# An adaLN transformer block on one core: the opening's loads on two queues, its first products by feature halves, and seven block products for one more head

## The reference

```python
ada = cond @ ada_w + ada_b                       # six 256-wide chunks per sequence
x1 = layernorm(x) * (1 + scale1) + shift1
q, k, v = split(x1 @ qkv_w + qkv_b)              # 16 heads of 128
a = softmax(q @ k.T / sqrt(128)) @ v
y = x + gate1 * (a @ out_w + out_b)
h = gelu((layernorm(y) * (1 + scale2) + shift2) @ ffn_w1 + ffn_b1)
z = y + gate2 * (h @ ffn_w2 + ffn_b2)
hn = rms_norm(square(relu(z @ ternary(W_fc).T)))
out = x + hn @ ternary(W_proj).T
```

## Time and profile before

| | |
|---|---|
| median of 3 runs | 350.53 us (349.86 to 351.02) |
| profiled execution | 350.69 us, span 348.9 us |
| TensorE busy | 342.3 us, 98% of the span |
| VectorE busy | 222.4 us, 64% |
| ScalarE busy | 220.2 us, 63% |
| GpSimd busy | 148.7 us, 43% |
| mean DMA rate | 47 GB/s over the span |

### The profile page before, as it was taken

The page is one execution under the profiler, slowest core; times in us unless marked ns, Lnnn a source line. Parts: engine busy times, 40 slices in busy tenths (PEclk is TensorE's granted clock), DMA queues, the critical chain, the costliest instruction groups (busy, mean ns, idle before and its releaser), DMA issues.

```text
span 348.9 us, 5879 instructions
## 1 busy us (share of the span) xinstructions
PE 342.3 (98%) x1950; PEld 293.7 (84%) x1950; DVE 222.4 (64%) x386; ACT 220.2 (63%) x560; POOL 148.7 (43%) x140
## 2 busy tenths in 40 slices
PE   8999999999999999999999999999999999999995
PEld 7888888889888888888888888888787788889884
DVE  6676756553555664456466454585875788577796
ACT  2773565667576657756664675667579536876593
POOL 3571329736534964644595573479341100000000
PEclk9999999999999999999999999999999999999998
DMA  6953003100300320030020002020000000000002
GB/s 176 362 192 120 3 0 120 62 1 3 120 0 0 120 60 0 0 120 0 25 95 0 0 6 115 0 62 0 4 0 2 0 2 0 0 2 1 1 32 90
DMA packets 12338, 16.53 MB, mean 47 GB/s; under 512 B 720, under 2 KB 8992, under 8 KB 12320
## 3 DMA queue, kind: packets, MB, share of 16 engines
q1 hardware_dynamic: 12136, 16.16, 14.2%
q10 hardware_dynamic: 184, 0.15, 0.1%
HBM read 15.25 MB, written 1.05 MB: 47 GB/s over the span
## 4 chain that ended last, share of the span: by engine, by line
PE 74%; issue 20%; DVE 3%; ACT 1%; POOL 1%; POOLq 0%; ACTq 0%
PE bank L1228 16%; PE bank L1230 16%; PE bank L1229 16%; PE bank L1315 8%; PE bank L1298 8%; PE bank L1304 4%; PE bank L1427 2%; PE bank L1442 1%; DVE yT L976 1%; DVE yT L966 1%; PE bank L1463 1%; PE bank L1422 1%; DVE yT L962 0%; ACT prob L579 0%; ACT hbuf L718 0%
## 5 line engine op out<-in xcount | busy, mean ns | idle before, releaser
L391 POOL TENSOR_TENSOR prob<-prob,rinv 128x512 f32<-128x512 f32 x32 | 36.2, 1131 | 60.3 <-DVE rinv L1025 59.9
L579 ACT ACTIVATE prob<-bank,negmax 128x128 f32<-128x128 f32 x128 | 45.4, 365 | 25.6 <-DVE negmax L1012 25.6
L1315 PEld LDWEIGHTS bank<-probT,vals 128*128 128x128 f32 x256 | 33.3, 191 | 3.2 <-issue 0.8
L952 DVE SCALAR_TENSOR_TENSOR o_lo<-bank,bias,o_hi 128x512 fp32r<-128x512 f32 x32 | 23.9, 745 | 17.2 <-ACT o_hi L532 17.2
L532 ACT ACTIVATE o_hi<-bank,bias 128x512 fp32r<-128x512 f32 x32 | 21.9, 686 | 19.4 <-PE bank L1315 19.4
L1315 PE MATMUL bank<-probT,vals 128*128 128x128 f32 x256 | 33.9, 275 | 0.0
L350 POOL TENSOR_TENSOR wqk_lo<-raw_qk,wqk_hi 128x512 fp32r<-128x512 f32 x16 | 21.2, 1323 | 19.6 <-ACT wqk_hi L493 18.1
L488 POOL TENSOR_TENSOR xr<-raw_qk,xt 128x256 f32<-128x256 f32 x1 | 0.7, 721 | 67.2 <-ACT raw_qk L796 67.2
L1012 DVE TENSOR_REDUCE negmax<-bank 128x4 f32<-128x512 f32 x32 | 21.8, 682 | 7.9 <-PE bank L1298 7.9
L1228 PE MATMUL bank<-wv_hi,x_hi 128*128 128x512 f32 x62 | 26.1, 420 | 0.0
L579 ACT ACTIVATION_READ_ACCUMULATOR prob<-bank,negmax 128x1 f32 x128 | 26.0, 203 | 0.0
(11 more groups left out here) (218 smaller groups left out, 974.1 us busy)
## 6 DMA issues: line engine op xcount, KB each, us to landing
raw_qk<-in_L_cond_qkv_w_dram SPq DMA_DIRECT2D x6, 512.0 KB, 4.6
raw_v<-in_L_cond_qkv_w_dram SPq DMA_DIRECT2D x4, 512.0 KB, 4.1
raw_o<-in_L_cond_out_w_dram SPq DMA_DIRECT2D x4, 512.0 KB, 3.5
t_w<-in_L_cond_ada_w_dram SPq DMA_DIRECT2D x1, 1024.0 KB, 8.9
raw_w<-in_L_cond_ffn_w_dram SPq DMA_DIRECT2D x2, 512.0 KB, 6.9
t_raw<-in_L_ffn_W_fc_dram SPq DMA_DIRECT2D x4, 256.0 KB, 3.7
t_raw<-in_L_ffn_W_proj_dram SPq DMA_DIRECT2D x4, 256.0 KB, 3.8
raw_qk<-in_L_cond_ffn_w_dram SPq DMA_DIRECT2D x1, 1024.0 KB, 4.9
```

Source lines behind the costliest of these rows:

```text
L391: nc.gpsimd.tensor_tensor(e, e, rinv[:, j % 2, :].unsqueeze(2).broadcast_to([P, SQ, P]), ALU.mult).then_inc(norm_done, 1)
L579: e = nc.scalar.activation(prob[:, j % 2, s, :], bank[BS][:, s * P:(s + 1) * P], ACT.Exp, bias=negmax[:, j % 2, s:s + 1], accum_out=rowsum ...
L952: nc.vector.scalar_tensor_tensor(out=lo[:, :], in0=bank[BO][:, :], scalar=bias[:, bass.ds(HG * G + VB + j % HG, 1)], in1=hi[:, :].bitcast( ...
L1315: m = nc.tensor.matmul(bank[BO][:, s * P:(s + 1) * P], vals[:, b, h], probT[:, s, :], start=True, stop=True)
```

## The change

The three parts:

1. **Opening.** The second half of quad 0's x is loaded from ScalarE's queue, and the bias rows too; SyncE then waits for the first half alone. The identity matmuls go from 5 + 7 + 3 to 5 + 3 + 1, and TensorE transposes all bias rows before the conditioning product. Transposes come by feature half (k = 1 first), VectorE modulates sequences 0 and 1 and ScalarE sequences 2 and 3 of each half, and queries and keys of head 0 are made together, half by half. One of two `wv_lo` parts and one of two copies of raw x move to VectorE.
2. **First group.** Head 2's queries and keys are made by the seven products. `weight_sums` takes two heads at once, `x_sums` moves ahead of unit (0, 1), and the two `x_sums_lo` stand together.
3. **End of attention.** The addition of x becomes `add_x`, a step of its own, announced by half. For quad 1 the gate, the addition and the transposes are spread over later chunks; `transpose_y` goes half by half.

```diff
         @block.sync
-            for h in range(2):
-                s = slice(h * SQ // 2, (h + 1) * SQ // 2)
-                sp.dma_start(xt[:, s, :], x[s].rearrange("b t d -> t b d")).then_inc(x0_in[h], 16)
+            sp.dma_start(xt[:, 0:SQ // 2, :], x[0:SQ // 2].rearrange("b t d -> t b d")).then_inc(x0_in[0], 16)
             sp.dma_start(ada_w1, ada_w[:, 0:2 * D].rearrange("(k p) n -> p k n", p=P)).then_inc(ada1_in, 16)
-            sp.wait_ge(x0_in[1], 16)
+            sp.wait_ge(x0_in[0], 16)
...
         @block.gpsimd
             pool.wait_ge(xs_lo, KD)
-            for k in range(KD):
-                wv_lo_part(k, k + 1)
+            wv_lo_part(0, 1)
             wqk_lo_part(1, 2)
...
-            weight_sums(0, 3, 4, 0)
+            weight_sums(0, 2, 4, 0)
...
         @block.scalar
+            act.dma_start(xt[:, SQ // 2:SQ, :], x[SQ // 2:SQ].rearrange("b t d -> t b d")).then_inc(x0_in[1], 16)
             act.dma_start(crow, cond).then_inc(cond_in, 16)
             act.dma_start(arow, ada_b.rearrange("(n p) -> n p", p=P)).then_inc(arow_in, 16)
+            for src, at, n in ((qkv_b, QB, 3 * H), (out_b, OB, KD), (ffn_b1, F1B, NC), (ffn_b2, F2B, KD)):
+                act.dma_start(brow[at - NA:at - NA + n, :], src.rearrange("(n p) -> n p", p=P)).then_inc(bias_in, 16)
...
         @block.vector
+            def modulate_first():
+                dve.wait_ge(ada_ready, 1)
+                for k, src, full, hi in ((1, bank[BO], m1_d, hi1_d), (0, bank[BV], mod_d, hi0_d)):
+                    dve.wait_ge(xt0_done, KD - k)
+                    for b in range(SQ // 2):
+                        m = nc.vector.tensor_scalar(xq0[:, k, b * P:(b + 1) * P], src[:, b * P:(b + 1) * P],
+                                                    ada[:, SCALE1 + k, b:b + 1], ada[:, SHIFT1 + k, b:b + 1], ALU.mult, ALU.add)
+                    m.then_inc(full, 1)
+                    dve.wait_ge(full, 1)
+                    nc.vector.tensor_copy(x_hi[:, k, 0:SQ // 2 * P], xq0[:, k, 0:SQ // 2 * P]).then_inc(hi, 1)
...
-            modulate(0, SHIFT1, SCALE1, bank[0:2])
-            dve.wait_ge(small_cp, 4)
+            modulate_first()
+            dve.wait_ge(wv_h, 2)
+            nc.vector.tensor_tensor(wv_lo[:, 1, :], raw_v[:, 1, :], wv_hi[:, 1, :].bitcast(F32), ALU.subtract).then_inc(wv_l, 1)
+            dve.wait_ge(xraw_mm, 1)
+            nc.vector.tensor_copy(xT[:, 1, cols(0)], bank[BS][:, :]).then_inc(xT1_done, 1)
+            dve.wait_ge(small_cp, 3)
             keep_q0(0, 0, 1)
...
                 if c == 1:
                     accumulate(NU - 1, NG - 1, 1, last=True)
+                if c == 2:
                     gate_y(1)
-                if c == 5:
+                if c == 3:
+                    add_x(1)
+                if c == 6:
                     dve.wait_ge(gt_mm, 2)
                     stats_of(3)
...
         @block.tensor
+            def first_qk():
+                dsts = (bank[BQ], bank[BK])
+                pe.wait_ge(wqk_h, 1)
                 for k in (1, 0):
...
-            ada_product(GATE1 + 4, GATE1 + 6, ada_w2, bank[7])
             pe.wait_ge(q1_done, 1)
             pe.wait_ge(k1_done, 1)
-            qk_products(2, 0, 0)
+            pair_p1(0, 2)
+            pair_p2(0, 2)
+            ada_product(GATE1 + 4, GATE1 + 6, ada_w2, bank[7])
+            pair_p6(0, 2)
+            pair_p5(0, 2)
+            pair_p7(0, 2)
             ada_product(GATE1 + 6, GATE1 + 8, ada_w2, bank[7])
-            pe.wait_ge(q1_done, 2)
-            pe.wait_ge(k1_done, 2)
-            qk_products(2, 0, 1, (BE, BY))
+            pair_p4(0, 2)
+            pair_p3(0, 2)
```

More of the change, by code:

```diff
@@ L524, in modulate @@
                 hi_part(x_hi[:, 0, cols(quad)], xf[:, 0, :], xs_hi)
-                if e:
-                    act.wait_ge(mod_d, e + 1)
-                    hi_part(x_hi[:, 1, cols(quad)], xfull[:, 1, :], xs_hi)
+                act.wait_ge(mod_d, e + 1)
+                hi_part(x_hi[:, 1, cols(quad)], xfull[:, 1, :], xs_hi)
+            def modulate_first():
+                act.wait_ge(ada_ready, 1)
+                for k, src, full, hi in ((1, bank[7], m1_a, hi1_a), (0, bank[6], mod_a, xs_hi)):
+                    act.wait_ge(xt0_done, KD - k)
+                    for b in range(SQ // 2, SQ):
+                        m = nc.scalar.activation(xq0[:, k, b * P:(b + 1) * P], src[:, b * P:(b + 1) * P], ACT.Identity,
+                                                 bias=ada[:, SHIFT1 + k, b:b + 1], scale=ada[:, SCALE1 + k, b:b + 1])
+                    m.then_inc(full, 1)
+                    act.wait_ge(full, 1)
+                    hi_part(x_hi[:, k, SQ // 2 * P:SQ * P], xq0[:, k, SQ // 2 * P:SQ * P], hi)
             def biased_hi(hi, psum, at, ready, count, hi_sem):
@@ L1073, in _ @@
             modulate(1, SHIFT1, SCALE1, bank[6:8])
+            x_sums()
             unit(0, 1)
             keep_qk1(0, 0, 3, BQ, BK)
[L1076 removed]
+            x_sums_lo(0)
+            x_sums_lo(1)
             keep_qk1(1, 0, 4, BE, BY)
[L1078 to L1080 removed]
+            pair_q0(0, 2)
+            pair_k1(0, 2)
             ada_part(1, GATE1, NA, bank[7])
[L1082 removed]
+            pair_q1(0, 2)
             with dve.Fori(0, NG - 1) as G:
@@ L1472, in _ @@
             transpose_raw(0, (bank[BE], bank[BS]))
-            keep_awake(3)
-            def first_query():
+            def first_qk():
+                dsts = (bank[BQ], bank[BK])
                 pe.wait_ge(wqk_h, 1)
-                for k, ready in ((1, x01_hi), (0, xs_hi)):
-                    pe.wait_ge(ready, 1)
-                    nc.tensor.matmul(bank[BQ][:, :], wqk_hi[:, k, 0:P], x_hi[:, k, cols(0)], start=k == 1, stop=False)
-                pe.wait_ge(wqk_l, 1)
                 for k in (1, 0):
-                    nc.tensor.matmul(bank[BQ][:, :], wqk_lo[:, k, 0:P], x_hi[:, k, cols(0)], start=False, stop=False)
-                for n, k in enumerate((1, 0)):
-                    pe.wait_ge(xs_lo, n + 1)
-                    m = nc.tensor.matmul(bank[BQ][:, :], wqk_hi[:, k, 0:P], x_lo[:, k, cols(0)], start=False, stop=k == 0)
-                m.then_inc(q_mm, 1)
+                    if k:
+                        pe.wait_ge(hi1_d, 1)
+                        pe.wait_ge(hi1_a, 1)
+                    else:
+                        pe.wait_ge(hi0_d, 1)
+                        pe.wait_ge(xs_hi, 1)
+                    for w in (wqk_hi, wqk_lo):
+                        if w is wqk_lo:
+                            pe.wait_ge(wqk_l, 1)
+                        for n in range(2):
+                            nc.tensor.matmul(dsts[n][:, :], w[:, n * KD + k, 0:P], x_hi[:, k, cols(0)],
+                                             start=k == 1 and w is wqk_hi, stop=False)
+                for k in (1, 0):
+                    pe.wait_ge(xs_lo, KD - k)
+                    for n, done in ((0, q_mm), (1, k_mm)):
+                        m = nc.tensor.matmul(dsts[n][:, :], wqk_hi[:, n * KD + k, 0:P], x_lo[:, k, cols(0)], start=False, stop=k == 0)
+                        if k == 0:
+                            m.then_inc(done, 1)
             def first_values():
@@ L1537, in transpose_y @@
             def transpose_y(quad):
-                pe.wait_ge(gated, quad + 1)
-                for s in range(SQ):
-                    for c in range(KD):
+                for c in range(KD):
+                    pe.wait_ge(gated, KD * quad + c + 1)
+                    for s in range(SQ):
                         m = nc.tensor.transpose(bank[BACK[quad][s // 2]][:, (s % 2) * D + c * P:(s % 2) * D + (c + 1) * P],
```

134 lines of the change are left out of this document (62 added, 72 removed).

## The result

The changed kernel takes **353.41 us** in the median of five executions (352.98 to 354.35), the kernel before 349.88 beside it: ratio 1.0095, 95% interval 1.0076 to 1.0114. By the ratio, which takes in all executions, it is slower by 3.3 us (3.5 between the medians), where I had forecast no change, and it lies outside the range. The profiled execution took 352.98, the shortest of the five, with a span of 351.2, 2.3 more than that of before.

What follows compares the result with a forecast made beforehand. TensorE, busy 98% of the span, was taken to bound the kernel. +0.5 us at the loop's start and -0.6 at the end gave 350.5 us against 350.53; own range 349.7 to 351.2, over the cases 349.0 to 352.0.

Steps and rivals of the forecast that it cites:

- the opening gains 0.3 us: Opening: conditioning product 0.52 us earlier, less 2.3 passes more at the slow clock; gain 0.3 us, not 0.5.
- the fast clock comes later: Rival, opening: TensorE's full clock rises only behind the transposes; 1.1 us later than forecast, 351.6 us; chance 0.14.
- the row of biases and cond: Opening: conditioning row 0.4 us later behind x, bias transposes 0.3 us; product starts at about 7.0 instead of 7.52.
- the race: Opening: VectorE's wv_lo part against GpSimd's; forecast took VectorE first; rival GpSimd first costs 1.27 us, 351.8 us, chance 0.22.
- the halves' gain: Opening: head 0's queries and keys end a microsecond earlier; TensorE 0.65 us ahead at quad 1's transposes.
- turns of VectorE and GpSimd in the first group: First group: six VectorE operations alternate with 3.0 us of GpSimd work; VectorE through at 30.1, negmax 2.2 us late.
- The lead survives: Rival, first group: VectorE's sums and GpSimd don't take turns, stalls vanish; 1.4 us gained in all, 349.1 us; chance 0.27.
- The stall at the value product: First group: transposed probabilities come at 31.35 where TensorE wants them at 30.85; 0.55 us stall.
- head 2: First group: stalls of 0.25 and 0.65 us at p6 and p5, 0.55 in joins; loop's scores 0.5 us later, 42.9.
- the end: End of attention: quad 0 gains 0; quad 1 closes two holes, 0.6 us saved.
- two mishaps together: Two of the unfavourable cases both happening; said to lie outside the range over the cases, 349.0 to 352.0 us.

Runs made afterwards that it cites:

- the fillers alone: The changed kernel with the old front (old loads, bias transpose behind the first products) but its own fewer identity matmuls: 353.08 us, ratio 1.0063 to the kernel before.

## Why the prediction was wrong

- **Failed: "the opening gains 0.3 us".** I took the clock to stay as it was and priced 2.3 passes more at the slow level. It was the rival "the fast clock comes later" that happened, with chance 0.14. Its mechanism was right and its size too small: I had the product at "about 3 us" and four transposes slow, 1.1 in all; measured are 3.42 us, all eight transposes slow and the modulation 1.5 us late where I had it 0.3 early, 1.8 in all, of which the next point has 0.36. The transposes of raw x were slow too, up to 13.93. I gave it little since I read the trace of before as one that had much filler to spare. The experiments show that it had little: taken from the start or from ahead of the product, fewer identity matmuls made most executions 2 us and more longer, and the traces of two such executions (the changed kernel, the fillers alone) have the late clock. Which place matters more stays open. The Trainium skill ("TensorE: Matmul & The Clock Gate", Part 1) says that the throttled state is the default and activity releases it, and that the number of slow matmuls differs between runs of one kernel; the traces here agree (rises at 5.6, 7.1, 7.9 and 8.4 us in kernels with the old loads and identity matmuls, and two groups of times in four kernels).
- **Failed: the row of biases and cond.** I put the product at 7.0, it came at 7.36. The landing of cond cost 0.4 as taken. The identity passes took 0.26 us each (six from 4.66 to 6.23) and the last two 0.3, where I had 0.224, and the bias transposes 0.54 where I had 0.3.
- **Failed: the race, and the halves' gain.** I took VectorE first; GpSimd was first by 0.17 us, and by 0.16 or 0.17 in every trace with that code. Counted from the modulation's start, `x_lo` ended at 3.23 us where I had 3.4, and ScalarE's second `wv_hi` at 3.44 where I had 3.3. The turns held (1.67 us is about 1.29 and 0.65, less the head start), the price didn't: 1.27 forecast, about 0.4 measured with the early clock; with the late one no gain was seen, in runs whose clocks differ. I had said that nothing hides it; the waits ahead of the first query hide most. From the modulation to quad 1's transposes I had 9.96 us, 0.36 less than before, and it took 11.04: 1.08 more than forecast: the race has 0.28 of it, and the rest is that the halves, which I had as a gain of 0.36, cost 0.44 there. With the 1.8 ahead of it these are all of the 2.87 us between my 20.0 and the 22.87 measured.
- **Right: turns of VectorE and GpSimd in the first group.** From the first `x_lo` to the end of the sums I had 6.6 us (23.5 to 30.1), and the trace has 6.28 (26.27 to 32.55). The Trainium skill ("SBUF — State Buffer", "Who interferes with whom") calls the shared pair of ports an exclusive lock, for which a VectorE instruction with two inputs in SBUF and a GpSimd instruction that reads SBUF contend. The rows above agree: VectorE's operations of 0.7 us last 1.52 and 1.75 while GpSimd works, and 0.7 again behind it, and GpSimd's of 0.73, 1.04 and 1.29 last 1.21, 1.49 and 1.71. "The lead survives" is out. The stall at the value product, 0.55 forecast, doesn't show: TensorE was late by then itself, and started it at 33.81, 0.06 behind VectorE's copy of the probabilities.
- **Right in its sum: head 2.** From p1 to the scores I had 7.85 us and the trace has 45.48 - 37.56 = 7.92. Stalls of 0.5 ahead of p5, 0.2 ahead of p4 and 0.5 ahead of the scores (distances between starts, less the matmuls between them) stand for my 0.65 and 0.55; the 0.25 at p6 wasn't there. What I missed is that the 0.5 us lost here isn't set off by a gain in the opening: alone, the scheme costs 0.7 at the scores in its trace and 1.2 over all executions.
- **Right: the end.** Quad 0 nothing (0.14), quad 1 0.6: measured 0.7 together, in the run with the end alone.
- **The range.** I left out "two mishaps together". Clock and race both come from the same part of the change and both happened; with my own prices they give 350.5 + 1.1 + 1.3 = 352.9. The range should have reached there, and 353.41 would have been outside even so. That this sum comes near is partly luck: its clock is too cheap and its race too dear.

## What to carry to other kernels

Matmuls without a use ahead of a product with few columns are part of the schedule: before they are taken out, look at what else runs on TensorE until the clock has risen, and time several executions, since one profile shows only one of them. Cases against a forecast that come from one part of a change need not be independent, and the range must hold them together. And a change of three parts is best timed part by part: here the new end gained 0.7 us, the halves cost 0.6, and the front and head 2's products cost most.

## What the runs showed that I had not expected

- The granted clock can fall again early: up at 5.97, down at 9.39 during transposes that follow 16 matmuls of 8 columns, up at 12.8. In that profile TensorE waited for nothing longer than 0.4 us between 1.52 and 14.
- With fewer identity matmuls one kernel has two groups of times, by execution, with medians 2.3 to 3.7 us apart (0.7 to 1.1%) in three kernels, and 2.0 in the changed kernel with two more of them at the start. With all fifteen and the old loads the kernel before had one group in 92 executions.
- The row `arow`, on one queue behind 256 KB of x and cond, landed at least 2.4 us later than with cond alone ahead of it.
